# Output projection of an attention and expert kernel: one fp32 product against three fp32r products of high and low parts

## What is computed

```
q, k, v = x @ Wq + bq, x @ Wk + bk, x @ Wv + bv      # 8 heads of 64 features
feats   = softmax(q k^T / sqrt(8)) v                 # per head
x1      = layernorm(x + feats @ Wo + bo)             # Wo: 512 x 512, the output projection
shared  = silu(x1 @ Wsu_gate) * (x1 @ Wsu_val) @ Wsd
scores  = sigmoid(x1 @ w_gate); top 6 of 64 experts per token, up to 256 tokens per expert
routed  = weighted sum over the 6 of (silu(.) * (.)) @ w_down[e]
out     = layernorm(x1 + shared + routed)
```

## Time and profile before

| | us |
|---|---|
| median of 3 runs (1292.84 to 1294.88) | 1293.24 |
| span of the profiled execution, first to last instruction | 1289.5 |
| median of the runs less that span | 3.7 |
| PE busy | 1255.7 (97%) |
| DVE busy | 998.2 (77%) |
| ACT busy | 919.8 (71%) |
| POOL busy | 513.2 (40%) |

### The profile page before, as it was taken

One profiled execution on the slowest core, in us unless ns is written; L12 is line 12 of the kernel. 1 busy time (PEld: TensorE's weight loads), 2 busy tenths in 40 slices (PEclk: granted clock), 3 DMA queues, 4 the chain that ended last, 5 costly groups with the idle time before them and its releaser, 6 DMA issues. The chain is left out here.

```text
span 1289.5 us, 24161 instructions
## 1 busy us (share of the span) xinstructions
PE 1255.7 (97%) x8128; PEld 1058.8 (82%) x8128; DVE 998.2 (77%) x1891; ACT 919.8 (71%) x1643; POOL 513.2 (40%) x508
## 2 busy tenths in 40 slices
PE   7999999999999999999999999999988999999896
PEld 5888799889889889989989989989866877777642
DVE  5623688789889979979979979979866777776387
ACT  5421589778878868868868868878833877778343
POOL 0002223234524524524533533542543666676412
PEclk9999999999999999999999999999999999999999
DMA  8788466212424424323423423543578999997698
GB/s 282 258 283 289 155 196 223 69 42 84 147 66 138 145 70 139 125 88 110 146 84 101 155 89 88 156 136 120 178 272 326 386 386 385 346 339 252 237 426 335
DMA packets 90951, 253.14 MB, mean 196 GB/s; under 512 B 16824, under 2 KB 39480, under 8 KB 87504
## 3 DMA queue, kind: packets, MB, share of 16 engines
q1 hardware_dynamic: 70608, 196.78, 44.9%
q0 software_dynamic: 17920, 50.62, 10.2%
q10 hardware_dynamic: 2304, 4.20, 0.8%
HBM read 177.87 MB, written 134.91 MB: 243 GB/s over the span
## 5 line engine op out<-in xcount | busy, mean ns | idle before, releaser
L967 ACT ACTIVATE p_hi<-slot 128x512 fp32r<-128x512 f32 x512 | 278.5, 596 | 108.9 <-PE slot L1594 105.5
L807 POOL TENSOR_TENSOR p_lo<-prob,p_hi 128x512 fp32r<-128x512 f32 x128 | 166.1, 1297 | 441.9 <-ACT prob L969 441.7
L1607 PE MATMUL slot<-k_stack,q_stack 128*128 128x512 f32 x1024 | 300.1, 415 | 0.0
L984 ACT ACTIVATE prob<-prob,row_min 128x1024 f32<-128x1024 f32 x256 | 296.8, 1160 | 0.1
L1307 DVE TENSOR_TENSOR p_lo<-slot,p_hi 128x512 fp32r<-128x512 f32 x384 | 250.8, 681 | 52.5 <-ACT p_hi L967 51.1
L1594 PE MATMUL slot<-ident,prob 128*128 128x128 f32 x2048 | 265.8, 273 | 1.3 <-ACT prob L984 1.3
L1632 PE MATMUL pv_acc<-p_hi,v_pair 128*128 128x256 f32 x1024 | 263.1, 290 | 2.6 <-POOL p_lo L807 1.8
L1632 PE MATMUL pv_acc<-p_lo,v_pair 128*128 128x256 f32 x1024 | 253.7, 281 | 0.0
L1594 PEld LDWEIGHTS slot<-ident,prob 128*128 128x128 f32 x2048 | 229.5, 141 | 1.9 <-issue 1.7
L1632 PEld LDWEIGHTS pv_acc<-p_hi,v_pair 128*128 128x128 f32 x1024 | 192.6, 188 | 16.1 <-issue 5.7
L1632 PEld LDWEIGHTS pv_acc<-p_lo,v_pair 128*128 128x128 f32 x1024 | 192.8, 188 | 12.9 <-issue 3.3
(11 more groups left out here) (196 smaller groups left out, 1974.4 us busy)
## 6 DMA issues: line engine op xcount, KB each, us to landing
disp_hbm<-zero_hbm SPq DMA_DIRECT2D x64, 518.0 KB, 6.3
rows_all<-disp_hbm SPq DMA_DIRECT2D x64, 518.0 KB, 12.8
y_hbm<-zero_hbm SPq DMA_DIRECT2D x48, 512.0 KB, 4.4
got<-y_hbm SPq DMA_DIRECT2D x15, 1536.0 KB, 19.0
q_stack<-q_hbm SPq DMA_DIRECT2D x128, 128.0 KB, 3.1
up_pair<-in_L_ffn_w_up SPq DMA_DIRECT2D x26, 512.0 KB, 9.5
down_w<-in_L_ffn_w_down SPq DMA_DIRECT2D x32, 256.0 KB, 12.0
q_hbm<-q_hi SPq DMA_DIRECT2D x8, 512.0 KB, 2.7
```

The source lines that it names most:

```text
L807: e.tensor_tensor(p_lo[1][:, 2:4, :], prob[:, m % 2, :, (4 * u + 2) * P:(4 * u + 4) * P], p_hi[1][:, 2:4, :].bitcast(F32), ALU.subtract).t ...
L967: e.activation(p_hi[b][:, two, :], view[:, two, :], ACT.Copy).then_inc(a_phi, 1)
L984: e.activation(keys, keys, ACT.Exp, bias=row_min[:, me % 2, j, 1:2], scale=-1.0, accum_out=row_sum[:, me % 2, j, half:half + 1]).then_inc( ...
L1607: made = e.matmul(slot[:, n * BANK:(n + 1) * BANK], qs[:, part, j * P:(j + 1) * P], k_stack[:, ms % H, keys], start=part == 0, stop=part == 1)
```

## The change

`feats @ Wo` is made by `three_products`, 12 fp32r products of 512 columns for a tile, where it was 4 fp32 products (8 in the trace). `Wo` is split once, in four pieces of 128x512: ACT writes `wo_hi` at steps 6 to 9, DVE `wo_lo` at steps 7 to 10, from `wo_raw`, into which the DMA of step 4 now goes (it waits for the last low parts of the values too, since `wo_raw` lies over them). The features are split per pair of heads: `feats` holds one pair; ACT writes `feats_hi` (`high_feats`) 17 steps after the pair's first step, DVE `feats_lo` (`low_feats`) one step later, the last pair's behind the attention loop. POOL's join waits for the low part of the pair before. The ticks of the chunk's end are later: `out_project` 11 and 15 (5 and 9 before), `P0` 18 (14), `P1` 41 (38). `zeros` and `code_of` share their places with others; the pool for POOL's descriptors is 4096 bytes of a partition.

```diff
-        wo_sb = sb("wo_sb", [P, KC, C], F32, att)
+        wo_hi = sb("wo_hi", [P, KC, C], F32R, att)
+        wo_lo = sb("wo_lo", [P, KC, C], F32R, att)
-        feats = sb("feats", [P, H // 2, QC], F32, att)
+        feats = sb("feats", [P, QC], F32, att)
+        wo_raw = sb("wo_raw", [P, KC, C], F32, wo_first)
+        feats_hi = sb("feats_hi", [P, H // 2, QC], F32R, att)
+        feats_lo = sb("feats_lo", [P, H // 2, QC], F32R, att)
...
-        P0, P1 = 14, 38
+        P0, P1 = 18, 41
+        def split_tick(s, late):
+            pair, wait = divmod(s - STEPS - 13 - late, 2 * STEPS)
+            return range(pair, pair + 1) if wait == 0 and 0 <= pair < NCH * H // 2 - 1 else range(0)
...
# SP, step 4
                 if s == STEPS:
                     e.wait_ge(v_vadd, NS)
-                    e.dma_start(wo_sb[:, :, :], Wo[:, :, :]).then_inc(d_wo, 16)
+                    e.wait_ge(v_vlo, NS)
+                    e.wait_ge(g_vlo, NS)
+                    e.wait_ge(a_vhi, 2 * NS)
+                    e.dma_start(wo_raw[:, :, :], Wo[:, :, :]).then_inc(d_wo, 16)
...
# POOL, the join
-                    e.wait_ge(p_proj, 2 * (mj // H))
+                    e.wait_ge(v_flo, mj // 2)
...
# ACT
+            def high_feats(pair):
+                head_out(e, 2 * pair)
+                head_out(e, 2 * pair + 1)
+                e.wait_ge(v_wosplit, KC)
+                e.wait_ge(p_proj, 2 * (pair // KC))
+                e.activation(feats_hi[:, pair % KC, :], feats[:, :], ACT.Copy).then_inc(a_fhi, 1)
...
+                if 6 <= s < 6 + KC:
+                    e.wait_ge(d_wo, 16)
+                    e.activation(wo_hi[:, s - 6, :], wo_raw[:, s - 6, :], ACT.Copy).then_inc(a_wosplit, 1)
+                for pair in split_tick(s, 0):
+                    high_feats(pair)
...
+            high_feats(NCH * H // 2 - 1)
             attention_over(e)
# DVE
+            def low_feats(pair):
+                e.wait_ge(a_fhi, pair + 1)
+                e.tensor_tensor(feats_lo[:, pair % KC, :], feats[:, :], feats_hi[:, pair % KC, :].bitcast(F32),
+                                ALU.subtract).then_inc(v_flo, 1)
...
+            while jobs:
+                side_step(jobs)
+            low_feats(NCH * H // 2 - 1)
             attention_over(e)
# PE
             def out_project(c, j):
-                e.wait_ge(d_wo, 16)
-                head_out(e, c * H + H - 1)
-                head_out(e, c * H + H - 2)
+                e.wait_ge(v_wosplit, KC)
+                e.wait_ge(v_flo, KC * (c + 1))
                 wait_misc(reads_of(c, j))
-                for k in range(KC):
-                    made = e.matmul(bank_of(c, j)[:, :], feats[:, k, j * P:(j + 1) * P], wo_sb[:, k, :],
-                                    start=k == 0, stop=k == KC - 1)
-                made.then_inc(p_proj, 1)
+                cols = slice(j * P, (j + 1) * P)
+                three_products(bank_of(c, j)[:, :], [lambda k: feats_hi[:, k, cols], lambda k: feats_lo[:, k, cols]],
+                               [lambda k: wo_hi[:, k, :], lambda k: wo_lo[:, k, :]], p_proj)
...
             def chunk_end(c):
                 to = ticks()
-                yield from to(5)
+                yield from to(11)
                 out_project(c, 0)
-                yield from to(9)
+                yield from to(15)
                 out_project(c, 1)
...
-    nc = _bacc.Bacc("TRN2", target_bir_lowering=False, num_devices=1)
+    nc = _bacc.Bacc("TRN2", target_bir_lowering=False, num_devices=1, dynamic_dma_scratch_size=4096)
```

More of the change, by code:

```diff
@@ L142, in build @@
         mean_var, rstd = (moments[:, 12:14], moments[:, 14:16]), (moments[:, 16:17], moments[:, 17:18])
+        fill = ExitStack()
+        zeros = sb("zeros", [P, ZW], F32, fill)
+        fill.close()
         class Routing:
@@ L194, in build @@
         row_at = sb("row_at", [P, 2 * E], U32, moe)
+        code_of = sb("code_of", [P, E], U32, moe)
         hit = [sb(f"hit{i}", [P, 2, 2, TOPK], U32, moe) for i in range(2)]
@@ L226, in build @@
         v_min, v_lo, v_sum, v_inv, v_scaled = (sem(f"dve_{n}") for n in ("min", "p_lo", "sum", "inverse", "scaled"))
+        a_wosplit, v_wosplit, a_fhi, v_flo = (sem(n) for n in ("act_wo_hi", "dve_wo_lo", "act_feats_hi", "dve_feats_lo"))
+        g_codes = sem("pool_codes")
         v_resid, v_norm = sem("dve_resid"), sem("dve_norm")
@@ L569, in sync @@
             load_w(KC)
[L570 removed]
+            e.dma_start(bv_all[:, :], bv.partition_broadcast(P)).then_inc(d_bv, 16)
             load_w(KC + 1)
@@ L760, in chunk_end @@
                 to = ticks()
-                yield from to(10)
+                yield from to(15)
                 root(c, 0)
-                yield from to(P0 + 1)
+                yield from to(P0 + 2)
                 root(c, 1)
@@ L830, in gpsimd @@
             attention_over(e)
+            e.iota(code_of[:, :], [[CODE_E, E]], base=CODE_0, channel_multiplier=0).then_inc(g_codes, 1)
             jobs = [last_end(END)]
@@ L1275, in chunk_end @@
                 to = ticks()
-                yield from to(6)
+                yield from to(12)
                 add_resid(c, 0)
-                yield from to(8)
+                yield from to(14)
                 measure(c, 0)
-                yield from to(10)
+                yield from to(16)
                 add_resid(c, 1)
-                yield from to(12)
+                yield from to(17)
                 measure(c, 1)
@@ L1335, in vector @@
                         accum_out=row_min[:, ms % 2, j, half:half + 1]).then_inc(v_min, 1)
+                if 7 <= s < 7 + KC:
+                    e.wait_ge(a_wosplit, s - 6)
+                    e.tensor_tensor(wo_lo[:, s - 7, :], wo_raw[:, s - 7, :], wo_hi[:, s - 7, :].bitcast(F32),
+                                    ALU.subtract).then_inc(v_wosplit, 1)
+                for pair in split_tick(s, 1):
+                    low_feats(pair)
                 if s < V_LATE:
@@ L1366, in vector @@
                     pair, b = (f - SH) // 2, rows_of_item(f - 1)
+                    if pair == 0:
+                        e.wait_ge(g_codes, 1)
                     e.tensor_tensor(hit[pair % 2][:, :, :, :], rows_all[:, b:b + 2, :, C:WITH].bitcast(U32),
```

15 lines of the change are left out of this document (8 added, 7 removed).

## The result

The changed kernel takes 1331.73 us (median of 4 runs, 1330.19 to 1334.29), the kernel before 1293.04 beside it: ratio 1.0301, 95% interval 1.0286 to 1.0317. It is slower, as forecast, but by 38.7 us and not by 10.6, and outside the range. The span of the profiled execution is 1331.3 us (before 1289.5), 41.8 more.

A forecast was written before the change was run, and what follows sets the result against it. PE was taken to bound attention, and a chain of waits the part after it. Terms: -8.8 + 3.5 + 9.6 + 2.1 + 0.4 + 3.8 = +10.6 us, so 1303.8 us against 1293.24; range 1291 to 1308.

The forecast's parts named there:

- The projection: Output projection on PE: 12 new products take 2.80 us a tile instead of 3.43; 14 tiles within attention give -8.8 us.
- Rival 4: Projection's weight loads and products stream at half the distance: 1.4 us a tile, 28.4 us gained, about 1282; chance 0.02.
- Splitting Wo: Start of attention: ACT waits for Wo's DMA, then ACT and DVE do the pieces, making PE late: +3.5 us (1.7 to 5.6).
- (a): Attention, chunks 0 to 5: two scatters ahead of a join delay the features; PE waits 1.6 six times: +9.6 us (0 to 16).
- (b): First tile's expert scores: ACT's exponential now shares a step with PE's spread, 0.3 late seven times: +2.1 us.
- (c): Last steps of attention, where ACT is full: pair 30's part delays them by its 0.39: +0.4 us.
- Elsewhere I find no loss.: Rest of attention, beyond the three exceptions by place: measuring and normalizing keep their order, so no cost.
- room of about 0.3: Measuring and normalizing on DVE: claimed slack of about 0.3 us against PE's transposes, so no loss there.
- The end: Behind attention: ACT waits for the last feats DMA, delaying the 24 products by 4.66: +3.8 us (2.5 to 4.7).

The follow-up runs named there:

- x7: The changed kernel with the second tile's scatters half a step later (`P1 + 21` instead of `P1 + 20`): ratio 1.0189 to the kernel before.
- x10: The changed kernel with only the second tile's weights on DVE a step later (`P1 + 30` instead of `P1 + 28`): ratio 1.0311 to the kernel before.
- x12: The changed kernel with DVE's measuring of the second tile one and a half steps later, behind the first tile's normalizing: ratio 1.0230 to the kernel before.
- x3: The changed kernel with the first tile's normalizing, transposes and routing one step later (`P0` 20 instead of 18): ratio 1.0515 to the kernel before.
- x6: The changed kernel with POOL's `p_lo` on 32 of 256 columns, part of the computation left out: ratio 1.0124 to the kernel before.
- x4: The changed kernel with the last pair's high and low parts behind the first of the shared expert's rows' parts: ratio 1.0253 to the kernel before.
- x5: x2 plus last pair's parts behind the third rows' parts, Wo split later (low parts on GpSimd), second pairs' low part and first bias later: ratio 1.0108.
- x8: The kernel before with only the scratch for GpSimd's DMAs set to 4 KB: ratio 1.0010 to the kernel before.
- x2: The changed kernel with all side work of a chunk exactly four steps later than in the kernel before: ratio 1.0041 to the kernel before.

## Why the prediction was wrong

By its own steps:

- The projection: 12 starts from 263.14 to 265.71, so 2.80 us with the last; right to the hundredth. Rival 4 is out.
- Splitting Wo: +3.5 forecast, +3.15 measured. ACT was idle for 2.21 before the first part (2.6 forecast); each part took 0.63 to 0.68. (The upper bound given, 5.6, counts the first part twice; by its own terms it is 4.8.)
- (a): +9.6 forecast; six times 1.30, 7.8 (8.9 with the 0.2 at place 12). ACT waits 2.24 where I had 2.7. x7 and x10 together isolate it.
- (b): +2.1 forecast; seven waits, the step 0.35 longer, 2.4.
- (c): 0.4 forecast, 0.2 measured.
- **"Elsewhere I find no loss."** This is the step that failed: it put at nothing what lost some 29 us (30.2 in attention, plus 8.8 of gain, less 7.8 and 2.4). The order of DVE's measuring and normalizing is the same as before, as I wrote, but I took that for the whole of it. Two things follow from the places and not from the order.
  - Place 16, 1.7 a chunk, 12 in all: adding, measuring and normalizing come in two steps between the projection and the transposes, where three were; the "room of about 0.3" was read where three were. Measuring elsewhere gives back 8 of them (x12). A step more ahead of the transposes alone gives nothing back (x3), so it is rather the pile on DVE that costs than the distance; what makes up the rest was not tried.
  - The places 0, 4 and 8, 2.2 a chunk in six chunks, 13 in all: operations of about 0.17 us wait for POOL, at place 4 since the features' low part stands ahead of them. x6 shows it for 0 and 4 by POOL's length. For 8 the trace alone speaks (`row_inv` 1.79 us, inside POOL's bias and `p_lo`).
  - Of what is left, 1.8 is a single meeting of the same kind: at 838.08 normalizing started 0.06 behind POOL's `p_lo` and took 1.51 where it takes 0.53. Some 2 us lie in places of 0.1 to 0.2.
- The end: +3.8 forecast, +6.6 measured. The mechanism was right (4.6 us late); of the 2.8 by which the term was mis-sized, 2.2 are what the 24 products lost at the lower clock. I had priced them at the duration of the earlier trace rows without asking what PE's longer idle time does to it.

The terms that I had priced came to +11.4 us in the trace (with the gain of 8.8 as forecast), near the 10.6, so the direction was no luck; what I had put at nothing was more than twice as large.

The trace of before could have told me. There, `weight_of` already had a mean of 339 ns where its shortest is 144, and `row_inv` was longer than its shortest in all 51 cases in which it started inside an operation of POOL (counted as above). The prediction has no term for the routing's small operations; a mean at over twice the minimum was the sign that they wait.

Still open: in the traces of x4, x5 and x8 the first addition after attention starts 2.7, 2.8 and 1.9 us behind the projection that it needs, and I can't name what it waits for there.

## What to carry to other kernels

When side work is moved in a pipeline with a period, move it by whole periods, on all engines, with its loads; x2 undid 34 of 39 us by that alone. For each small operation of VectorE ask what GpSimd runs at that moment: its price is 0.17 us or the rest of GpSimd's operation, with the next one of GpSimd if that follows without a gap (`weight_of` 2.0 us), and a start 0.04 us later can decide. Compare an operation's mean with its minimum before calling it free, and where a wait leaves TensorE idle ahead of a block of products, price the block at the lower clock too.

## What the hardware showed that I had not expected

The price of such a meeting is a cliff, not a slope: 0.17 us at 0.01 ahead, 1.28 at 0.03 behind, 0.32 at 0.03 behind a GpSimd operation of 0.32. On the edge it goes either way: in the kernel before, `row_inv` started 0.006 to 0.011 us behind one of POOL's joins eleven times and took 0.15 us in five of them, 0.73 to 0.75 in six. In x4 the cast was short in three chunks of seven and long in the rest, with nothing changed between them. And a wait of 2.0 us on one engine can cost nothing (x10), while one of 1.1 costs 0.85.
